# Pacing POOL's gathers in two edge passes of a graph kernel: one wait moved and one dropped in the wide pass, one added in the typed pass

## The reference

```python
# layer 0: relations. W[r] = sum_b comp[r,b] * basis[b]
msg = x[src] * edge_weight
s   = segment_sum(msg, etype * N + dst, R * N)          # then sum over r of s[r] @ W[r]
h   = relu(einsum('rni,rio->no', s, W) + bias)          # + relu(x @ res_w.T + res_b), batch norm

# layer 2: messages of width 128
msg_in   = concat([x[src], x[dst], edge_attr])          # 64 + 64 + 32
messages = relu(msg_in @ mW1 + mb1) @ mW2 + mb2
agg      = segment_sum(messages, dst)
out      = relu(concat([x, agg]) @ uW1 + ub1) @ uW2 + ub2

# layers 1 and 3: graph convolution with W1, W2; and sum over each node's in-edges of its own x
```

## Time and profile before

| | us |
|---|---|
| median of 3 runs | 13067.97 (13048.71 to 13082.49) |
| profiled execution, its own time | 13061.65 |
| its span | 13059.6 |
| typed pass, from the first gather | 565 to about 5650 |
| wide pass, from the first gather | 8170 to about 12951 |
| mean granted clock of PE | 0.754 of full speed |

### The profile page before, as it was taken

The page is one execution under the profiler, slowest core; times in us unless marked ns, Lnnn a source line. Parts: engine busy times, 40 slices in busy tenths (PEclk is TensorE's granted clock), DMA queues, the critical chain, the costliest instruction groups (busy, mean ns, idle before and its releaser), DMA issues. The chain is left out here.

```text
span 13059.6 us, 144784 instructions
## 1 busy us (share of the span) xinstructions
PE 7317.3 (56%) x52908; PEld 5611.8 (43%) x52956; DVE 6785.9 (52%) x8156; ACT 2833.4 (22%) x2654; POOL 6396.0 (49%) x6717
## 2 busy tenths in 40 slices
PE   9755545455555555469999998333333333333334
PEld 4333333333333333359998998222222222222223
DVE  5466666666666666652223223455544555445555
ACT  4333333333333333330000001111111111111112
POOL 4465565665665665610000000666666666666665
PEclk9866666667676766689999999666666666666667
DMA  9733332333332333349997997433333333333332
GB/s 389 307 100 104 104 100 99 109 100 104 105 100 99 109 100 103 106 173 369 371 370 289 370 370 269 97 93 96 91 92 92 93 95 92 92 92 92 95 93 65
DMA packets 480426, 2020.11 MB, mean 155 GB/s; under 512 B 193465, under 2 KB 246136, under 8 KB 354776
## 3 DMA queue, kind: packets, MB, share of 16 engines
q1 hardware_dynamic: 205304, 1283.59, 28.0%
q0 software_dynamic: 206272, 317.25, 10.4%
q10 hardware_dynamic: 68768, 418.23, 8.7%
HBM read 1385.92 MB, written 632.61 MB: 155 GB/s over the span
## 5 line engine op out<-in xcount | busy, mean ns | idle before, releaser
L428 POOL DMA_INDIRECT big<-Yd,ix x3223 | 3049.2, 946 | 2020.8 <-PE ps L535 1046.4
L1303 POOL DMA_INDIRECT big<-Pd,mt x3223 | 3048.9, 946 | 1806.9 <-issue 938.8
L527 PE MATMUL ps<-ring 128*128 128x490 bf16 x3223 | 1423.6, 537 | 2177.0 <-DVE ring L465 979.8
L462 DVE TENSOR_TENSOR ring<-ps,vw 128x2940 bf16<-128x2940 f32 (+1 forms) x516 | 1726.3, 3346 | 1723.3 <-PE ps L529 1305.9
L1332 DVE TENSOR_TENSOR ps<-ps,big 128x1024 f32<-128x1024 f32 x403 | 481.9, 1226 | 2341.4 <-DMA big<-Pd,mt 2341.4
L527 PEld LDWEIGHTS ps<-ring 128*128 128x128 bf16 x3223 | 412.4, 128 | 2971.2 <-issue 2098.1
L1439 PE MATMUL ps<-idt,total 128*128 128x128 f32 x135 | 64.0, 474 | 2459.4 <-issue 2398.4
L535 PE MATMUL ps<-big 128*65 128x128 f32 x6446 | 1135.3, 347 | 355.1 <-issue 354.3
L535 PEld LDWEIGHTS ps<-big 128*65 128x65 f32 x6446 | 1050.0, 186 | 444.9 <-issue 442.3
L549 ACT ACTIVATE Z<-ps 128x1470 bf16<-128x1470 f32 (+1 forms) x584 | 799.0, 1399 | 1780.0 <-remote 913.8
L549 ACT ACTIVATE big<-ps 128x1470 bf16<-128x1470 f32 (+1 forms) x576 | 787.2, 1398 | 1719.4 <-remote 924.1
(11 more groups left out here) (215 smaller groups left out, 11658.7 us busy)
## 6 DMA issues: line engine op xcount, KB each, us to landing
Yd<-big SPq DMA_DIRECT2D x196, 1024.0 KB, 8.8
Aj<-Z SPq DMA_DIRECT2D x65, 3062.5 KB
big<-Aj SPq DMA_DIRECT2D x130, 1531.2 KB, 8.4
cb<-Aj ACTq DMA_DIRECT2D x130, 1531.2 KB, 8.4
Aj<-big SPq DMA_DIRECT2D x64, 3062.5 KB
cb<-Aj SPq DMA_DIRECT2D x128, 1531.2 KB, 8.4
Z<-Aj ACTq DMA_DIRECT2D x128, 1531.2 KB, 8.5
dr<-in_dstr SPq DMA_DIRECT2D x135, 1152.0 KB
```

Of the source, the lines that this page charges most:

```text
L428: e.indirect_dma_start(gv[j][:, k, 0:64], None, table, bass.IndirectOffsetOnAxis(ap=ix[j][:, k:k + 1], axis=0)).then_inc(sm[f"g{j}"], 16)
L462: nc.vector.tensor_tensor(one[r][:, 0:m, :], bc_t(iof, m, W * NT), bc_f(vw[j][:, k], m, W * NT), ALU.is_equal)
L527: nc.tensor.matmul(PS[q][:, 0:W * NT], olo[r][:, c, :], one[r][:, c, :], start=True, stop=False)
L1303: e.indirect_dma_start(gv[j][:, k, :], None, Pd, bass.IndirectOffsetOnAxis(ap=mt[j][:, k:k + 1], axis=0)).then_inc(sm[f"g{j}"], 16)
```

## The change

In the wide pass the 13th gather of a block waits for p0, the block's first eight products, where it waited for p1; the 21st gather waits for nothing, where it waited for p2. In the typed pass, from block 1 on, the 20th gather of block b waits until cm1 has reached 3b. The `sem_inc` behind each wait is the kernel's way to tie a wait to an instruction of its own.

```diff
@@ typed_pass, gpsimd @@
                     e.wait_ge(sm["ix"], reg(e, b + 1))
                     e.sem_inc(sm["pool"], 1)
-                    for k in range(LA if at(b, NA - 1) else KA):
+                    first, last = at(b, 0), at(b, NA - 1)
+                    done = reg(e, 3 * b)
+                    for k in range(LA if last else KA):
+                        if k == 19 and not first:
+                            e.wait_ge(sm["cm1"], done)
+                            e.sem_inc(sm["pool"], 1)
                         e.indirect_dma_start(
@@ wide, gpsimd @@
                     for k in range(KL if last else K):
                         if k == 12:
-                            e.wait_ge(sm["p1"], n)
-                            e.sem_inc(sm["pool"], 1)
-                        if k == 20:
-                            e.wait_ge(sm["p2"], n)
+                            e.wait_ge(sm["p0"], n)
                             e.sem_inc(sm["pool"], 1)
                         e.indirect_dma_start(gv[j][:, k, :], None, Pd,
```

## The result

| | before | changed |
|---|---|---|
| median of 4 runs, us | 13068.14 (13048.71 to 13082.49) | 12754.99 (12751.88 to 12757.86) |
| ratio, with its 95% interval | 1 | 0.9762 (0.9750 to 0.9774) |
| profiled execution, us | 13061.65 | 12754.94 |
| typed pass, us | 5085 | 4875 |
| wide pass, us | 4781 | 4678 |

A forecast was written before the change was run, and what follows sets the result against it. A ring of waits paced the wide pass, with POOL's wait for p1 on its path. Terms -732 + 28 - 2 = -706 against 13061.65 gave 12,356, stated as 12,360; its own range 12,320 to 12,440, widened to 12,300 to 12,470.

The forecast's parts named there:

- What bounds the kernel: Wide pass: a ring of waits, POOL's gathers, their landing, DVE's additions; 35.30 us a block, with the p1 wait on its path.
- p0's readiness: Wide pass, 13th gather: PE's first products plus 0.79 let POOL go at 10027.47, so the block shown would not wait.
- The remainder that I put at 28 us: Wide pass: waiting for p0 that stays, mean 0.21 a block over 133 blocks, 28 us given back, bounds 0 and 82.
- 732: Wide pass: POOL's idle time behind PE that the change removes, 775.1 less gaps of 0.30, in us; 5.5 a block.
- Gathers at their pace: Wide pass: gathers 13 to 24, moved beside DVE's one-hot work, keep their durations; cost 0, upper end 32 us.
- The 21st gather: Wide pass: its wait for p2 is already met, so removing it gives 0.
- Cost 0: Typed pass: the 20th gather's wait for cm1 delays it about 0.2 us, covered by 26 us for the landing; 0 in all.
- B: Wide pass: every block waits for p0, 0.62 to 1.2 us, 82 to 160 back, 12,410 to 12,490; chance 0.10.
- C: Wide pass: POOL cannot keep its gather pace without a pause; 12,516, or up to 13,140, slower; chance 0.05.
- D: Typed pass: the added wait is for the gathered block's own eighth triple; 1060 us lost, 13,420, slower; chance 0.03.

The follow-up runs named there:

- typed-only kernel: Kernel before plus only the typed pass's 20th-gather wait for cm1: 11724.42 us, ratio 1.000, on chip A; 12822.61 on chip C, one run, no ratio.
- wide-only one: Kernel before with only the wide pass changed (13th gather waits for p0, none at the 21st): 11380.62 us, ratio 0.9706, on chip A.

## Why the prediction was wrong

**What bounds the kernel** held. The ring from POOL's gathers through their landing to DVE's additions sets the wide pass in every kernel and on every chip that I ran, but for the two on chips C and D in which POOL pauses too shortly or not at all, and the time gained per block is the time that POOL no longer idles.

**The step that failed** is p0's readiness: "with the 0.79 seen between p1 and the gather, POOL could go at 10027.47, ahead of 10027.74". It took PE's recorded end plus 0.79 for the moment at which POOL can act on the signal. The 0.79 had been read at the one place where it is true on that chip: p1 ended at 10032.42, when POOL had already stood still for 4.99. The wait for p1 had hidden a hold of about 4.2 and 0.79 behind itself. With p0 that hold is bare. The remainder that I put at 28 us (0.21 a block) measured 659.9 less 131 gaps of 0.30, 621 us; 732 - 621 = 111 is what that leaves of the gain, and the pass lost 103. The trace of the kernel before records the raise of p0 that the forecast needed: 10031.68 in the block of the earlier trace rows, 5.00 after the products, and only 0.76 before p1's (10032.44). Over the 134 blocks p1 was raised 101 us after p0 in all. That is the gain that this wait had to give, and the pass gave 103. On chip A the same step gives the time: 487.0 us of idle time behind PE in the typed-only kernel became 138.2 in the wide-only one, 349 less, and the time fell by 345. My formula had said blocks of 30.0 to 30.7; they are 30.70.

**Gathers at their pace** held (943 ns, and 0.30 to the next). The Trainium skill's rule on DVE locking POOL out (DMA: Bandwidth & Descriptors, section SWDGE vs HWDGE vs iDMA), which I had set against the rows, did not show: in the kernel with no wait on chip A DVE's one-hot instructions (3.35 us each) run beside gathers in every block, and the gathers keep 943. Whether DVE runs these instructions in the two-port mode no run here shows, so the rule itself is not put to the test. What was held up was something else: PE's signals, beside POOL's gathers.

**The 21st gather**: free, as said: gathers 13 to 24 keep their pace in the changed kernel. Dropping the other wait as well is another matter: on chip C the kernel with neither is slower than before.

**The typed pass**: "Cost 0" put at nothing a term of 210 us in the other direction, and "PE and DVE neither gain nor lose an instruction" was true of instructions but not of their times. In the kernel before PE's sums ran beside the train's last gathers. Its timeline:

```profile
3059.43 0.94 POOL L428 DMA_INDIRECT big<-Yd,ix  x1 [0.30 <-issue]
3060.63 0.27 PE L535 MATMUL ps<-big 128*65 128x128 f32 x1 [0.64 <-issue]
...
3062.76 0.27 PE L535 MATMUL ps<-big 128*65 128x128 f32 x1 [1.86 <-issue]
...
3064.16 2.63 PE L535 MATMUL ps<-big 128*65 128x128 f32 x22 [0.38 <-issue]
3064.19 2.10 ACT L549 ACTIVATE Z<-ps 128x1470 bf16<-128x1470 f32 x2 [9.05 <-remote]
```

The train ended at 3060.37. Up to 3.8 later PE gets single matmuls, 2.1 apart; then 22 in a row, and at the same moment ACT is released, for which it had waited 9.05. With the pause at the 20th gather the hold is let go before the sums, which are in PE's critical exchange with DVE and ACT. By line, L535's idle time "issue" was 354.3 us before; the 2.4 of L540 above is what is left. Of these 352 us, 210 reached the end of the pass. That this edit alone does it is shown by the typed-only kernel on chip C (blocks 37.72 apart against 39.8, 266 us by one run). That the kernel is faster by as much as 313 is luck as far as the forecast goes: two thirds of it came from a part from which none was forecast.

**The rivals.** B, p0 as the ring's wait in every block, happened, but with a price of 0.62 to 1.2 it was sized by the clock and not by the hold; C and D did not happen. My expectations also missed after that: the typed wait at the 16th gather brought 0.7 us a block where I had expected several, because a second train held the sums' signal in its turn.

**What could have been read beforehand.** The waits of the kernel before held it:

```profile
ACT big L549 <- remote: 924.1, 118, 9.8
ACT Z L549 <- remote: 913.8, 112, 14.6
...
DVE ring L462 <- remote: 348.2, 97, 17.7
```

On one core there is no remote core. 2186 us of waits with no releaser in sight say that signals arrive when no recorded instruction ends. The recorded raises say the same of the one signal that mattered: p0's came a median 4.8 us after its products, and late in 133 of 135 blocks, before anything was changed. And ACT's issue of the `qw` loads took 1.34 us in the first wide block and 2.90 in the one of the earlier trace rows:

```profile
8212.06 1.34 ACTq L1392 DMA_DIRECT2D qw<-Qd  x2
...
10023.67 2.90 ACTq L1392 DMA_DIRECT2D qw<-Qd  x2
```

**Open.** Why chip A shows no hold and the others do. Whether it is the signal, the instruction stream of PE, or one cause for both: the runs show both together. Loading of code does not look like the cause, since the queues for instructions moved only five packets in the whole wide pass of the changed kernel and seven in the typed. That the signal is held apart from the work is shown by products that ended microseconds apart and were signalled within 0.1 us of each other: 121 such pairs in the typed pass before, with ends 4.0 apart in the median, and none on chip A. No experiment took the gathers' descriptors from POOL, which would tell whether issuing or writing them does it.

## What to carry to other kernels

Before moving a wait to an earlier signal, find a place in the trace where that signal is seen while the waiting engine has been busy all along; a delay that is read behind a long pause says nothing of one without it. "Remote" releasers on one core and single matmuls with idle time called "issue" beside a long train of indirect gathers mean that the recorded end of an instruction is not the time of its signal: there a pause of 3 to 5 us in a train, put where the held engine needs it most, can pay for itself, while one of 1.7 us or none may be slower. If the trace records when semaphores were raised, compare those times with the ends of the instructions before anything else. And a ratio from one chip is not that of another: removing the wait altogether is the best on chip A (0.9622) and worse than before on chip C (1.0169), so on both kinds the changed kernel or the one with the typed wait at the 16th gather (0.9704 and 0.9664) is the choice.

## What the runs showed of the hardware

- The same kernel took 11,726 us on one chip and 13,047 to 13,089 on three others, at much the same mean granted clock (0.753 to 0.759 on A, 0.748 to 0.756 on the others).
- On those three and on the first, signals of PE whose products end late in a train of gathers are raised only after it: p0 4.06 to 4.27 us after the last gather (medians, waits at the 13th and 17th gather), the typed pass's cm1 3.3 to 3.5. A waiting gather starts 0.77 behind the raise. In the typed pass of the kernel before, signals of the first 15 us of a train are on time.
- A pause of 1.7 us in the train does not end the hold; those of 3.4 and 5 us do.
- 3223 indirect gathers of 128 rows, back to back, keep 943 ns and a gap of 0.30, without any rest (chip A, no wait). In the blocks shown DVE starts on the landed rows 2.5 to 2.7 us after the last gather's start.
